# Two message layers of a graph network on one core: sums kept in SBUF by one-hot products instead of a scan and a scatter

## The reference

```
layer 0: m   = relu(concat(h[src], h[dst]) @ W_msg + b_msg)        # one message per edge
         agg = segment_sum(m, dst) / max(count(dst), 1)
         x   = x + relu(concat(h, agg) @ W_upd + b_upd)
layer 1: deg = max(count(dst), 1)
         agg = segment_sum(h[src] * deg[src]**-0.5 * deg[dst]**-0.5, dst) + h
         x   = x + agg @ W.T + b
```

## Time and profile before

| | us |
|---|---|
| median of 3 runs (6394.44 to 6401.90) | 6400.34 |
| the profiled execution | 6366.83 |
| its span, from the first to the last instruction | 6365.1 |
| busy: PE / DVE / ACT / POOL | 3175.8 / 2714.7 / 902.5 / 3206.7 |
| stage from, to: sort 40, 910; first_norm 910, 1047 | 870; 137 |
| edge sums 0 1047, 1913; update 0 1913, 2264 | 866; 351 |
| edge sums 1 2264, 2858; update 1 2858, 3175 | 594; 317 |
| attention 3175, 4093; update 2 4093, 4898; diffuse 4898, 6365 | 918; 805; 1467 |

### The profile page before, as it was taken

How to read it: one execution, slowest core, us unless ns; L and a number is a source line. 1 busy time by engine, 2 the same in 40 slices (tenths; PEclk the granted TensorE clock), 3 DMA queues, 4 the chain that set the end, 5 groups by cost and what they waited for, 6 DMA issues and landing times. The chain is left out here.

```text
span 6365.1 us, 56036 instructions
## 1 busy us (share of the span) xinstructions
PE 3175.8 (50%) x11306; PEld 1716.5 (27%) x11306; DVE 2714.7 (43%) x7289; ACT 902.5 (14%) x1499; POOL 3206.7 (50%) x2810
## 2 busy tenths in 40 slices
PE   4445421222228922226556666587773566655534
PEld 3113110111116711114312222255552222222212
DVE  6445445111114522215634444367776444444423
ACT  0000002000002200001112121133332111111110
POOL 0553542666661146663266666412221777777651
PEclk8555555555555555555555555555555666666665
DMA  7100013111116611115511111112211222223220
GB/s 300 43 1 3 1 49 122 22 22 22 22 19 174 204 44 21 21 19 209 197 21 20 21 20 21 60 57 84 85 75 62 28 29 28 29 27 28 27 19 4
DMA packets 351842, 360.21 MB, mean 57 GB/s; under 512 B 270280, under 2 KB 291856, under 8 KB 351778
## 3 DMA queue, kind: packets, MB, share of 16 engines
q1 hardware_dynamic: 209858, 264.03, 12.4%
q0 software_dynamic: 127088, 70.78, 8.3%
q10 hardware_dynamic: 14832, 24.70, 1.0%
HBM read 177.72 MB, written 188.20 MB: 57 GB/s over the span
## 5 line engine op out<-in xcount | busy, mean ns | idle before, releaser
L1968 POOL DMA_INDIRECT out<-d_out,d_end x356 | 588.4, 1653 | 172.2 <-issue 163.6
L434 POOL DMA_INDIRECT agg<-e_out,e_end x400 | 394.2, 986 | 271.3 <-DVE e_out L480 139.1
L2012 PE MATMUL d_pl<-d_hot,d_fields 128*65 128x512 f32 x712 | 516.5, 892 | 0.0
L476 DVE TENSOR_TENSOR_SCAN e_scan<-e_pk,e_scan,e_msg 65x512 f32<-65x512 f32 (+1 forms) x100 | 127.7, 1277 | 711.1 <-ACT e_msg L535 289.7
L1715 POOL DMA_INDIRECT half_sorted<-s_recs,s_place x200 | 191.9, 960 | 308.6 <-DVE s_place L1642 253.5
L1702 PE MATMUL s_within<-s_first_hi,identb 100*128 100x256 bf16 x400 | 159.5, 399 | 338.8 <-DVE s_hots L1621 281.4
L522 PE MATMUL e_pr<-ident,e_scan 65*128 65x65 f32 (+1 forms) x400 | 71.2, 328 | 481.5 <-DVE e_scan L476 285.1
L1628 DVE CUSTOM_DVE_ANT_0 s_picked<-s_within,s_hots 128x256 f32<-128x256 f32 x400 | 169.7, 425 | 326.0 <-remote 140.6
L424 POOL DMA_INDIRECT e_ends<-h,e_src x200 | 190.8, 954 | 228.0 <-DMA e_dst<-in_dst_ext 144.6
L1715 POOL DMA_INDIRECT list<-s_recs,s_place x200 | 191.4, 957 | 212.9 <-DVE s_place L1644 156.7
L638 POOL DMA_INDIRECT agg<-a_out,a_end x200 | 200.2, 1001 | 181.6 <-DVE a_out L813 115.7
(11 more groups left out here) (331 smaller groups left out, 8233.6 us busy)
## 6 DMA issues: line engine op xcount, KB each, us to landing
agg<-s_zeros SPq DMA_DIRECT2D x28, 896.0 KB
u_z<-h SPq DMA_DIRECT2D x28, 896.0 KB, 7.8
x<-u_t SPq DMA_DIRECT2D x28, 896.0 KB, 8.2
...
```

Of the source, the lines that this page charges most:

```text
L434: pool.indirect_dma_start(agg[:, :], bass.IndirectOffsetOnAxis(ap=end[s][:, j:j + 1], axis=0), out[s][:, j, :], None, bounds_check=NP - 1, ...
L1968: pool.indirect_dma_start(net.out[:, :], bass.IndirectOffsetOnAxis(ap=end[s][:, j:j + 1], axis=0), out[s][:, j, 0:C], None, bounds_check=N ...
L2012: last = nc.tensor.matmul(pl[0:WEIGHT + 1, :], fields[:, j, :], hot[:, j, :], start=j == 0, stop=j == J - 1)
```

## The change

**Order of rows.** All node tables are laid out by lane and tile: with node = 128 x tile + lane, the row is 392 x lane + tile (`TILES` = 392). `rows_of` takes from each partition's 392 rows the 28 of the chunk. The host permutes `x` and the output to match. The attention and the sort use row numbers in this order.

**plan_items**, a new stage ahead of the sort. The edges are sorted by target, so the pairs (edge block of 128 edges, node tile of 128 nodes) that have edges in common form a staircase of at most 392 + 200 - 1 steps. The stage computes for each step, called an item, its block, its tile, the chunk that must have been gathered, and for each of the block's edges the lane that it has in the tile (a number outside 0 to 127 where its target is in another tile), and writes these to HBM. Items are handled in lots of seven (`LOT`), 86 lots (`LOTS`).

**first_norm** also multiplies every node's h with both halves of `W_msg`, adds the bias to the second, and stores `from_src` and `from_dst` beside `h0`. Here `w_ends` holds the two halves side by side, once for partitions 0 to 63 and once for 64 to 127.

**edge_sums** keeps `sums`, 128 lanes by 392 tiles by 65 or 64 columns, in SBUF. POOL gathers whole chunks of messages and in layer 0 adds the two ends; ACT applies the relu, or in layer 1 the scale. DVE makes one-hot matrices (edge by lane) for the seven items of a lot, PE multiplies each with its block's messages, and DVE adds each product into `sums` at the item's tile, whose number is in a register. There is no scan, no flag and no scatter. The index loads per chunk are gone too.

**node_update** of layers 0 and 1 reads the aggregates from `sums` and writes the new x in their place, from where it is stored; it has no load of `agg`.

**sort_by_source** clears one aggregate table rather than three, and forms its keys from the new row numbers.

```diff
-    return table[bass.ds(chunk * (P * rows), P * rows), :].rearrange("(p g) c -> p g c", p=P)
-def first_norm(nc, net):
+    return table[0:NP, :].rearrange("(p n) c -> p n c", p=P)[:, bass.ds(chunk * rows, rows), :]
...
+            def _(pe):
+                pe.wait_ge(past_ready, 1)
+                for n, part in enumerate(parts):
+                    wide = part.stop - part.start
+                    for h in range(2):
+                        nc.tensor.matmul(spread_block[:, n, 0:wide], ones_f[:, :], past[h][:, part], start=h == 0, stop=h == 1)
+                    for h in range(2):
+                        last = nc.tensor.matmul(spread_dst[:, n, 0:wide], dst_f[:, h, :], inside[h][:, part], start=h == 0, stop=h == 1)
...
+                for h in range(2):
+                    nc.vector.tensor_scalar(past[h][:, :], numbers[0:HALF, :], finish_at[:, h, 0:1], None, ALU.is_gt)
+                    nc.vector.tensor_scalar(inside[h][:, :], numbers[0:HALF, :], finish_at[:, h, 1:2], None, ALU.is_gt)
+                v.drain()
+                for h in range(2):
+                    last = nc.vector.tensor_tensor(inside[h][:, :], inside[h][:, :], past[h][:, :], ALU.subtract)
+                last.then_inc(past_ready, 1)
...
+                for n, part in enumerate(parts):
+                    wide = part.stop - part.start
+                    nc.vector.tensor_scalar(block_of[:, part], spread_block[:, n, 0:wide], float(BLOCKS - 1), None, ALU.min)
+                v.drain()
+                nc.vector.tensor_tensor(tile_of[:, :], numbers[:, :], block_of[:, :], ALU.subtract)
+                v.drain()
+                for n, part in enumerate(parts):
+                    wide = part.stop - part.start
+                    nc.vector.scalar_tensor_tensor(lane_of[:, part], tile_of[:, part], float(-P), spread_dst[:, n, 0:wide], ALU.mult, ALU.add)
...
+                def from_dst(c, subs):
+                    r, s, h = c
+                    for i in subs:
+                        if i == 0:
+                            v.wait_ge(stored_e[s], 32 * h)
+                        v.wait_ge(src_out, SUBS * r + i + 1)
+                        bias = net.b_msg[:, :].unsqueeze(1).unsqueeze(1).to_broadcast([P, 2, 2, C])
+                        nc.vector.tensor_tensor(four(FD[s], i), end_rows((s + i) % 2, 1), bias, ALU.add).then_inc(dst_out, 1)
+                def step(c, done):
+                    if c is not None:
+                        centre(c)
+                    if done is not None:
+                        from_dst(done, range(0, 3))
+                    if c is not None:
+                        variance(c)
+                    if done is not None:
+                        from_dst(done, range(3, SUBS))
+                    if c is not None:
+                        scale(c)
+                step(at(0, 0), None)
+                with v.Fori(0, SUPER // 2 - 1) as t:
+                    for d in (1, 2):
+                        step(at(t, d), at(t, d - 1))
+                step(at(0, LAST), at(0, LAST - 1))
...
+                    if not (start and i < 2):
+                        pe.wait_ge(zt_ready, q - 1)
+                    pe.sem_inc(pe_turn, 1)
+                    for n in range(2):
+                        first = i * J + 2 * n
+                        last = nc.tensor.transpose(pt[b][:, n * P:(n + 1) * P],
+                                                   H[s][:, first:first + 2, :].rearrange("p j c -> p (j c)"), net.ident[:, :])
...
+                def step(c, start=False):
+                    r, s, h = c
+                    pe.wait_ge(normed, r + 1)
+                    turn(c, 0, start)
+                    for i in range(SUBS):
+                        q, b = SUBS * r + i, (s + i) % 2
+                        if i + 1 < SUBS:
+                            turn(c, i + 1, start)
+                        pe.wait_ge(zt_ready, q + 1)
+                        if not (start and i < 2):
+                            pe.wait_ge(dst_out, q - 1)
+                        pe.sem_inc(pe_turn, 1)
+                        for j in range(J):
+                            half, pair = slice(j % 2 * C, (j % 2 + 1) * C), j // 2
+                            last = nc.tensor.matmul(po[b][:, j % 2, pair * P:(pair + 1) * P], zt[b][half, pair * P:(pair + 1) * P], net.w_ends[half, :],
+                                                    start=True, stop=True)
+                        last.then_inc(mm_done, 1)
+                step(at(0, 0), True)
...
+                def square(c):
+                    r, s, h = c
+                    act.wait_ge(centred, r + 1)
...
+                def from_src(c, i, start):
+                    r, s, h = c
+                    q, b = SUBS * r + i, (s + i) % 2
+                    act.wait_ge(turned, q + 1)
+                    if not (start and i < 2):
+                        act.wait_ge(mm_done, q - 1)
+                    nc.scalar.activation(zt[b][:, :], pt[b][:, 0:2 * P], ACT.Copy).then_inc(zt_ready, 1)
+                    if i == 0:
+                        act.wait_ge(stored_e[s], 32 * h)
+                    act.wait_ge(mm_done, q + 1)
+                    nc.scalar.activation(four(FS[s], i), end_rows(b, 0), ACT.Copy).then_inc(src_out, 1)
+                def step(c, done, start=False):
+                    if c is not None:
+                        square(c)
+                    for i in range(SUBS):
+                        if done is not None:
+                            from_src(done, i, start)
+                        if i == 3 and c is not None:
+                            root(c)
+                step(at(0, 0), None)
+                step(at(0, 1), at(0, 0), True)
+                with act.Fori(0, SUPER // 2 - 1) as t:
+                    for d in (2, 3):
+                        step(at(t, d), at(t, d - 1))
...
+                            pool.indirect_dma_start(msg[:, b, 0:C], None, net.from_src[:, :],
+                                                    bass.IndirectOffsetOnAxis(ap=src[:, b:b + 1], axis=0)).then_inc(gathered[c % AHEAD], 16)
+                            pool.indirect_dma_start(near[c % 2][:, j, :], None, net.from_dst[:, :],
+                                                    bass.IndirectOffsetOnAxis(ap=dst[:, b:b + 1], axis=0)).then_inc(gathered[c % AHEAD], 16)
+                        else:
+                            pool.indirect_dma_start(msg[:, b, :], None, net.h1d[:, :],
+                                                    bass.IndirectOffsetOnAxis(ap=src[:, b:b + 1], axis=0)).then_inc(gathered[c % AHEAD], 16)
+                def add(c):
+                    pool.wait_ge(gathered[c % AHEAD], 16 * 2 * J * (c // AHEAD + 1))
+                    rows = msg[:, J * c:J * (c + 1), 0:C]
+                    nc.gpsimd.tensor_tensor(rows, rows, near[c % 2][:, :, :], ALU.add).then_inc(added, 1)
+                for c in range(CHUNKS):
+                    if two:
+                        if c > 1:
+                            pool.wait_ge(added, c - 1)
+                    elif c >= AHEAD:
+                        pool.wait_ge(msg_ready, c - AHEAD + 1)
+                    gather(c)
+                    if two and c > 0:
+                        add(c - 1)
+                if two:
+                    add(CHUNKS - 1)
...
+                    if two:
+                        act.wait_ge(added, c + 1)
+                        rows = msg[:, J * c:J * (c + 1), 0:C]
+                        nc.scalar.activation(rows, rows, ACT.Relu).then_inc(msg_ready, 1)
+                    else:
+                        act.wait_ge(gathered[c % AHEAD], 16 * J * (c // AHEAD + 1))
+                        for b in range(J * c, J * (c + 1)):
+                            last = nc.scalar.activation(msg[:, b, 0:C], msg[:, b, 0:C], ACT.Copy, scale=msg[:, b, C:C + 1])
+                        last.then_inc(msg_ready, 1)
...
+                if two:
+                    nc.vector.memset(msg[:, :, C:C + 1], 1.0).then_inc(cleared, 1)
+                nc.vector.memset(sums[:, :, :], 0.0)
...
+                v.sem_inc(summed, 2)
+                v.wait_ge(loaded, 16 * n_loads)
+                def one_hots(g, s):
+                    nc.vector.tensor_tensor(hot[s][:, :, :], lane[:, bass.ds(LOT * g, LOT)].unsqueeze(2).to_broadcast([P, LOT, P]),
+                                            numbers[:, :].unsqueeze(1).to_broadcast([P, LOT, P]), ALU.is_equal).then_inc(hot_ready, 1)
+                regs = [v.alloc_register(f"{n}tile{q}") for q in range(LOT)]
+                def add_up(g, s):
+                    v.reg_load(regs, tile_at[0:1, bass.ds(LOT * g, LOT)])
+                    tiles = [v.snap(r, min_val=0, max_val=TILES - 1) for r in regs]
+                    v.wait_ge(multiplied, g + 1)
+                    for q, tile in enumerate(tiles):
+                        to = sums[:, bass.ds(tile, 1), :].rearrange("p t c -> p (t c)")
```

(44 more changed lines are left out.)

531 lines of the change are left out of this document (292 added, 239 removed).

## The result

| | before | after |
|---|---|---|
| median of 4 runs each, us | 6399.15 (6394.44 to 6401.90) | 6732.51 (6727.13 to 6737.53) |
| ratio, 95% interval | | 1.0522 [1.0503, 1.0540] |
| profiled execution; its span | 6366.83; 6365.1 | 6733.06; 6731.3 |

The prediction was 6233, in a range of 6080 to 6340. It failed. On other chips the same two kernels came out level (0.998, in the experiments). The next table takes every stage from the first instruction in DVE's stream of it to the first of the next, in both traces; the forecast changes were reckoned from slightly other borders (first_norm 137, edge sums 864 and 592).

What follows compares the result with a forecast made beforehand. Each stage has its own bound, POOL's indirect DMAs in the edge sums; 1.5 + 33 + 2 + 283 - 296 - 3 - 164 - 24 = -167.5 us takes the profiled 6366.8 to 6199, moved by 33.5 to 6233, range 6080 to 6340.

Steps and rivals of the forecast that it cites:

- The step that failed: edge_sums layer 0: DVE's lots, 8.1 us per chunk, hidden beside POOL's 11.0; stage 568 us against 864, -296.
- R1: Rival, edge_sums: a lot's seven tile registers served in series on DVE, lot 7.3 us, whole 6551; chance 0.09.
- the two edge terms: edge_sums: layer 0 -296 us (-330 to -200), layer 1 -164 us (-250 to +60).
- first_norm: Stage with the new products per node: 420 us instead of 137, +283 (205 to 350).
- D: first_norm: time of a sub's products on PE, taken as 1.6 us, bounds 1.04 and 1.97.
- R2: Rival: first_norm's products side by side (1.04 us), -55; edge_sums items of 0.30 us, -95; whole 6083; chance 0.20.
- A sub: first_norm: one of seven steps per node chunk (PE transpose, ACT copy, four products, ACT copy), 2.67 us.
- the ring: first_norm: DVE's and ACT's serial work per node chunk outside the subs, 9.8 us of 28.5.
- update 1: node_update 1: one of three loads gone from a stage that waits on DMA, -24 us (-45 to 0).
- ACT's table cost: first_norm: ACT's table loads when Square, Sqrt and Copy alternate, 0 us, at worst +18.
- R3: Rival, edge_sums layer 0: each of POOL's 50 additions waits for a DVE comparison, +55 us, 6288; chance 0.15.
- R4: Rival: piecewise layout halves transfer rate in update 1 and diffuse, about +150 us, 6390, no change; chance 0.06.

Runs made afterwards that it cites:

- load_once: Changed kernel with the seven tile registers of DVE and PE loaded once ahead of the loop, not per lot: 6590.33 us.
- before_copy: The kernel before, unchanged, profiled on a chip without the hold-up: 5950.89 us.
- square_later: Changed kernel with first_norm's ACT square put behind the second sub-step and its copies reordered: 5810.53 us, 0.9782 of the kernel before.
- after_again: The changed kernel, unchanged, run again on a third chip: 5923.75 us, 0.9976 of the kernel before.
- the loop: Changed kernel with first_norm's ACT order edited and POOL's gathers in a loop, on a chip with the hold-up: 6322.95 us; edge 0 628.7, edge 1 687.3.

## Why the prediction was wrong

**The step that failed** is in edge_sums, layer 0: "Beside it DVE does 86 lots, 1.72 per chunk, at 4.7 (next part) = 8.1; hidden, with 2.9 to spare." The lot alone was sized well: 4.88 measured (comparison 1.09 as forecast; item 0.39 for 0.46; seven registers 1.62 for 0.3, of which the comparison covers most; 1.0 in all by load_once). But beside gathers it takes 28 to 40 us on these chips. POOL's 50 chunks and 69 of the 86 lots therefore come one behind the other: 565 + 347 where 568 in all was forecast. I had added durations of single instructions and checked only that no engine was full; the time from a product to the addition that waits for it, 59 us in the middle of these lots, stood in no row. In edge 1 the same hold-up leaves 78 of the 86 lots to run behind the gathers (261 + 425 us where 428 in all was forecast). Leaving the gathers out, or issuing plain loads, takes some 450 us away from edge 0 again: that the hold-up comes with POOL's indirect DMAs is shown, and that it shrinks with half of PE's records and not without the registers. R1 had the sign and a time of 6551, by luck: its rule that a lot decides from 6.4 us held, but registers in series were not the cause, and the lot alone stayed under it.

**The base of the two edge terms was too high as well.** I took 17.2 us a chunk as the cost of the work removed, of which 15.2 are POOL's issues. Before_copy shows that the stages of the kernel before were lengthened too: 787.7 instead of 880.1, 549.8 instead of 620.9 where the hold-up is absent. Where it is absent the change brings 787.7 - 598.6 = 189 in layer 0 and 549.8 - 466.3 = 84 in layer 1, against 296 and 164. The last 37 of layer 1's 466 are the lot (86 x 0.2 = 17) and what lies between the last addition and the next stage's first DVE operation (20, the timeline's idle ahead of L1469), which I had counted as 2.

**first_norm** was +218 for +283. D came out at 1.23, not 1.6: R2's half about the row halves was right and mine was not. A sub takes 2.07 and a node chunk 24.0 (forecast 28.5): 7 x 2.07, and 9.5 for the ring outside the subs against the 9.8 of the prediction. The ring was described rightly (ACT squares "and only then starts on the subs"), but I took it as fixed; square_later shows that 113 of the 218 us were that order and the copies' order within a sub.

**plan_items** 27.0 for 33, prepare +2.3 for +1.5, update 1 -26.3 for -24 with a gap on `u_x` of 134 instead of 182: right in kind and size. ACT's table cost stayed at nothing (one load, at L604). **R3**, POOL and DVE in each other's way, shows, but is cheap: POOL's addition takes 0.69 (0.46 forecast), and 0.94 in the middle, 1.56 at most, in the 5 of 50 that overlap a comparison, whose longest is 1.48 for 1.09; some 2 us in all. Without gathers 14 overlap, at 1.41. **R4** didn't show: update 2 and diffuse moved by -2.4 and +10.7; the attention's +12.5 is +0.7 without the hold-up. Update 0's +11 (10 on other chips too) and sort's +16 (9 there) I have not traced. Two readings were off without weight: POOL's 3206.7 of 6365.1 us is just over half of the span, and R4's +150 gives 6383, not 6390.

By chip then: without the hold-up +218 + 26 + 9 + 10 + 8 + 2 - 189 - 84 - 30 = -30, measured -27 between before_copy and after_again and -16.5 on one chip. Even there my -167 would have been six to ten times too much.

The Trainium skill ("Runtime: NRT & Kernel Launch", Instruction fetch mechanics) gives about 200 ns for each register that is loaded from HBM, in bulk too. Seven from SBUF in 1.62 us are 0.23 each here, so the trace agrees; an estimate by that figure would have put 1.4 in place of the 0.3 of my lot.

**What stays open.** What differs between chips (5930 to 5951 us for the kernel before on five, 6353 to 6413 on the others; each chip served at one time only, so a chip isn't told from its moment); what in POOL's indirect DMAs holds the products up, and why the loop's layer 0 escapes it. A pause in the written-out issues wasn't run on a chip that shows it. Every execution measured also carried a profile, which records each instruction; that recording has a part in the hold-up isn't excluded.
